# The attention stage of a transformer block: the counted loop over head groups written out as eight bodies in line

## What is computed

```python
mod = jax.nn.silu(condition) @ Wada + bada
sh_a, sc_a, gt_a, sh_m, sc_m, gt_m = jnp.split(mod, 6, axis=1)
xm = layernorm(x, g1, be1) * (1.0 + sc_a[:, None, :]) + sh_a[:, None, :]
x = x + gt_a[:, None, :] * attention(xm, Wqkv, Wproj, bproj)
xm = layernorm(x, g2, be2) * (1.0 + sc_m[:, None, :]) + sh_m[:, None, :]
h = gelu(xm @ W1 + b1)
return x + gt_m[:, None, :] * (h @ W2 + b2)
```

## Time and profile before

| | |
|---|---|
| median of three runs | 2285.84 us (2285.28 to 2287.09) |
| the profiled execution's own time | 2286.51 us |
| its span | 2284.5 us |
| PE busy | 2193.5 us (96% of the span) |
| DVE, ACT, POOL busy | 1293.9, 935.3, 846.0 us |
| mean granted PE clock | 0.978 of full speed |
| attention stage | about 348 to 1451 us of the span |

### The profile page before, as it was taken

The page is one execution under the profiler, slowest core; times in us unless marked ns, Lnnn a source line. Parts: engine busy times, 40 slices in busy tenths (PEclk is TensorE's granted clock), DMA queues, the critical chain, the costliest instruction groups (busy, mean ns, idle before and its releaser), DMA issues. The chain is left out here.

```text
span 2284.5 us, 36721 instructions
## 1 busy us (share of the span) xinstructions
PE 2193.5 (96%) x11550; PEld 1463.3 (64%) x11550; DVE 1293.9 (57%) x2872; ACT 935.3 (41%) x1780; POOL 846.0 (37%) x352
## 2 busy tenths in 40 slices
PE   6999999999999899999999999889999999999998
PEld 5888884444444445444454444577888888888886
DVE  4778876776777667676776765586323133133132
ACT  2111115555556555555555566444422222222221
POOL 2001008667578575785757773581000000000000
PEclk9999999999999999998999999999999999999999
DMA  6547446234261442614326231585211011010010
GB/s 228 208 154 254 145 160 148 48 90 103 53 136 46 92 91 53 149 39 98 79 53 149 50 88 52 181 286 201 92 56 56 0 55 55 0 55 30 25 37 18
DMA packets 129287, 223.46 MB, mean 98 GB/s; under 512 B 8526, under 2 KB 26006, under 8 KB 128920
## 3 DMA queue, kind: packets, MB, share of 16 engines
q1 hardware_dynamic: 107992, 179.38, 28.8%
q10 hardware_dynamic: 21120, 41.95, 5.0%
HBM read 146.31 MB, written 74.98 MB: 97 GB/s over the span
## 5 line engine op out<-in xcount | busy, mean ns | idle before, releaser
L1172 ACT ACTIVATE prob<-st 128x512 f32<-128x512 f32 (+3 forms) x1280 | 613.1, 544 | 431.1 <-PE st L1346 416.4
L1142 POOL TENSOR_TENSOR psum_k<-psum_k,prob 128x2048 f32<-128x2048 f32 x122 | 550.4, 4512 | 42.1 <-ACT prob L1172 34.7
L1228 DVE TENSOR_REDUCE part<-mx 128x1 f32<-128x512 f32 x708 | 435.8, 683 | 132.9 <-PE mx L1326 132.8
L1346 PE MATMUL st<-q_st,k_st 98*128 98x512 f32 (+3 forms) x1280 | 489.2, 397 | 16.5 <-issue 9.0
L1326 PE MATMUL mx<-k_st,qx_st 96*128 96x512 f32 (+3 forms) x1188 | 470.2, 415 | 18.6 <-DVE part L1224 13.3
L1346 PEld LDWEIGHTS st<-q_st,k_st 98*128 98x128 f32 x1280 | 245.7, 193 | 203.8 <-issue 115.5
L1740 DVE TENSOR_TENSOR m_g_lo<-m_g,m_g_hi 128x512 fp32r<-128x512 f32 x128 | 88.7, 693 | 495.3 <-ACT m_g_hi L1654 495.2
L1326 PEld LDWEIGHTS mx<-k_st,qx_st 96*128 96x128 f32 x1188 | 227.1, 192 | 169.2 <-DVE part L1228 96.9
L1224 DVE CUSTOM_DVE_ANT_0 unused<-mx,mask_row 128x128 bf16<-128x128 f32 x480 | 214.0, 488 | 148.7 <-PE mx L1326 131.5
L1363 PE MATMUL o_ps<-prob,v_sb 128*32 128x512 f32 (+3 forms) x2560 | 292.9, 564 | 0.0
L1650 ACT ACTIVATE m_g<-m_hid,vcol 128x512 f32<-128x512 f32 x128 | 88.3, 690 | 480.6 <-PE m_hid L1837 480.6
(11 more groups left out here) (168 smaller groups left out, 2608.1 us busy)
## 6 DMA issues: line engine op xcount, KB each, us to landing
k_st<-qk_scratch SPq DMA_DIRECT2D x96, 256.0 KB, 8.1
qx_st<-qk_scratch SPq DMA_DIRECT2D x96, 256.0 KB, 4.7
q_st<-qk_scratch SPq DMA_DIRECT2D x96, 256.0 KB
qk_scratch<-st_hi ACTq DMA_DIRECT2D x16, 1024.0 KB, 4.2
qk_scratch<-st_lo ACTq DMA_DIRECT2D x16, 1024.0 KB, 6.8
xs<-in_x_dram SPq DMA_DIRECT2D x8, 1024.0 KB, 8.4
v_sb<-v_scratch SPq DMA_DIRECT2D x8, 1024.0 KB, 15.8
o_scratch<-o_sb SPq DMA_DIRECT2D x32, 256.0 KB, 2.3
```

Of the source, the lines that this page charges most:

```text
L1142: nc.gpsimd.tensor_tensor(dst, src, prob[:, s % BUF, :, m:], ALU.add).then_inc(pool_added, 1)
L1172: nc.scalar.activation(prob[:, s % BUF, h, m:], st[n % RING][:, m:], ACT.Exp, scale=SCALE).then_inc(exp_done, 1)
L1228: nc.vector.tensor_reduce(most, bank[:, 0:w], AX.X, ALU.max).then_inc(mx_free, 1)
L1346: nc.tensor.matmul(st[n % RING][:, m:], k_st[u][0:MROWS, h, kt * P:(kt + 1) * P], q_st[0:MROWS, pos % 2, h, m:], start=True, stop=True).th ...
```

## The change

`per_group` no longer builds a loop. All eight bodies are written out one behind the other in every engine's stream, with `g` a constant, and the same `u`, `after` and `more` for each group as before. Nothing else is edited; lines below it are three lower in the changed file.

```diff
         def per_group(eng, body):
 
 
-            body(0, 0, False, True)
-            with eng.Fori(0, NG // 2 - 1) as i:
-                body(2 * i + 1, 1, True, True)
-                body(2 * i + 2, 0, True, True)
-            body(NG - 1, 1, True, False)
+            for g in range(NG):
+                body(g, g % 2, g > 0, g < NG - 1)
```

## The result

| | before | changed |
|---|---|---|
| median | 2285.56 us (2284.68 to 2287.09) | 2265.45 us (2264.21 to 2268.24) |
| ratio, 95% interval | | 0.9912 (0.9898 to 0.9925) |
| profiled execution, own time | 2286.51 us | 2268.24 us |
| its span | 2284.5 us | 2266.5 us |

The change takes 20.1 us off, where 12.0 were forecast. The profiled execution of the changed kernel is the slowest of its four runs, 2.8 us above their median, so the two traces show 18.0 us of the 20.1.

A forecast was written before the change was run, and what follows sets the result against it. PE was taken to bound the kernel, stalling for code at two back edges. Back edges -11.2, loop entry and exit -0.3, registers -0.5 sum to -12.0 us: median 2273.8 us, range 2270.0 to 2279.0.

The forecast's parts named there:

- What bounds the kernel, and where.: Attention: PE sets the pace; groups 3 and 5 stall 4.76 and 4.27 us at back edges, waiting for code.
- the rival that the stall belongs to the place: Start of groups 3 and 5: branch is cheap, the stall stays; 2284.7 us, no change; chance 0.06.
- The two back edges go: -11.2 us.: Groups 3 and 5 each lose 5.6 us, stall and lost clock, against a mean of 138.0; bounds -8.0 to -14.2.
- Nothing in the edit decides which [clock] a group gets.: Attention groups: whether one runs at mean clock 0.98 or 0.96 is untouched by the edit, so the mean was taken.
- The register instructions go: -0.5 us, bounds +0.4 and -1.3.: Groups 1 to 6: register instructions are hidden behind matmuls, at most 0.1 us per group in the mean.
- the sign that I had named: Last three chunks of a group clearly below 78 us at clock 0.98 would show the register instructions had an unseen price.
- The rival that "registers matter more": For example at ends of chunks: registers cost 1 us per group instead of 0.1, another 5.4 us, 2268.4 us; chance 0.02.
- The loop's entry and exit: -0.3 us.: Starts of groups 1 and 7: PE's step falls from 0.45 to 0.31 us, twice; between 0 and that.
- Code in line costs nothing.: Eight bodies instead of four, loaded in the background by the same two queues: no cost; a miss would cost 5.6 us.
- The slower rival: Each of six groups: in-line code arrives late on PE or SP, 5.6 us per group, +22.4 net, 2308.2 us; chance 0.04.

The follow-up runs named there:

- its repeat: The changed kernel, all eight bodies in line with constants, measured once more in a later series: 2265.74 us, ratio 0.9914 to the kernel before.
- the mirror kernel: Against the change: still in line without branches, but ACT, DVE, POOL and SP take groups 1 to 6 from registers, PE has constants; 2265.98 us, ratio 0.9915.

## Why the prediction was wrong

*What bounds the kernel, and where.* Right. PE sets the pace, groups 3 and 5 carry the stall, and it is a wait for code. One argument for it was misread: group 6 is followed by the code of group 7, not by "the same code" as group 0, so only group 0 spoke against the rival that the stall belongs to the place. The kernel with registers and no branch settles it, since its groups 3 and 5 start after 0.43 and 0.42 us.

*"The two back edges go: -11.2 us."* Right in mechanism, somewhat small: 13.6 us by the medians, 13.1 in the profiles. Groups 3 and 5 with registers and without a branch take 137.08 and 137.64 us, not the mean of 138.0 that I set against them. That is 12.5 us, and the other four groups together give the remainder of 0.7. It lies within the bounds I gave (-8.0 to -14.2).

*"Nothing in the edit decides which [clock] a group gets."* Wrong. Over all traces, and leaving out groups 3 and 5 where there is a back edge, 12 of 28 groups are at 0.96 with registers on PE (six kernels) and 5 of 44 with constants (eight kernels). In the change, its repeat and the mirror kernel it is one of 18. How the registers bring the clock down is not shown.

*"The register instructions go: -0.5 us, bounds +0.4 and -1.3."* **This is the step that failed.** They are worth 6.1 us. It failed in two ways, of about the same size. First, I stretched a price from three chunks over the fourth, which no in-line group of the old trace could show, since group 0's first chunk holds the start of the stage; the first chunks hold 3.2 us of the price. Second, I compared only groups of the same clock (0.98), and so left out groups 1 and 4, whose last three chunks take 79.7 and 79.8 us. These lose 1.4 and 1.5 us with the change, and with the registers kept they stay where they were; 2.9 us of the price lie in the last three chunks. So the earlier trace rows were read rightly, and the sign that I had named, a fall clearly below 78 us, did not show, because it looked at the one place and the one clock where the price is not. The term should have been left open over the first chunk, and its bound taken from what a group has there beyond matmuls, 58.71 us of time on 56.22 of PE work, 2.5 us per group. The rival that "registers matter more" had the size nearly right (1 us per group, 5.4 us), though not the place, and only 0.02 of the chance. With it my sum would have been about 2268. Why PE's registers cost at the group's start and at the diagonal tiles, and nowhere else at an equal clock, stays open.

*"The loop's entry and exit: -0.3 us."* Taken from 0.45 against 0.31, as if 0.31 were the floor. The floor is 0.18, since the 0.31 were registers too. Over the six steps that have registers that is about 1.2 us (0.13 to 0.27 each), part of the 6.1.

*"Code in line costs nothing."* Right. No engine has a new wait on "issue" of more than 0.3 us, and fewer packets of code are loaded. The slower rival did not occur, nor the one in which the branch is cheap. The case for PE as the only engine that matters was luckier than it was sound: I had only its wait in view, and ACT's 2.2 and DVE's 3.6 us stood hidden behind it.

The two pages of the Trainium skill divide as the rows had it. The wait for a target outside the loaded code, in the Trainium skill's page "Runtime: NRT & Kernel Launch", "Instruction fetch mechanics", is what the long loop shows, 4.3 to 4.8 us. The 108 ns of the Trainium skill's page "Advanced Engine Details and Errata", "Control Flow Timing", would have given no change; nearest to them comes the short MLP loop, at 0.56 us per pass over code in line, five times as much. That loop does stay loaded: neither code queue of the kernel before has a packet from 1800 to 2100 us, more than three of its passes.

## What to carry to other kernels

A loop whose body is too long to stay loaded pays at each branch back on every engine that runs it, side by side: take one engine's stall away and the next engine's shows, so change all the critical ones together before judging. A loop's price has a second part, the register instructions that its semaphore targets need; here they cost on the engine that sets the pace and on no other, half of it at few places and half through a lower clock. When the trace of before can't show a stretch without the suspected cost, that stretch belongs in the range with an open bound, not under the price of its neighbours. And where the suspected cause may move the clock, a comparison at equal clock leaves out a part of its price.

## What the runs showed of the hardware that was not expected

- At the same back edges PE waited 4.0 to 4.8 us for its code, DVE 3.5 to 3.6 and ACT 2.2 us (each seen where the longer waits had been taken away). POOL's and SP's never reached PE.
- A prefetch hint on the branch cut PE's wait from 4.0 to 4.8 down to 2.4 to 2.8 us, but with hints on all engines ACT then waited 7.59 us on "issue" once the loop had been left, and the sum was no gain.
- A PE register instruction is not free: 689 of them in two bodies, run three times, cost 6 to 7 us in all, some 3 ns each on average with what the clock loses, while those of ACT, DVE, POOL and SP together cost nothing that can be measured.
- One group of the attention took 134.12 us with a mean granted clock of 1.00 (and 134.13 in a second kernel), 2.4 us less than the usual 136.5 with 0.98. No run here tried to bring that about for every group.
- From the end of the attention to the MLP loop the same program text took 210.0 to 211.3 us in eleven kernels and 212.8 to 214.0 in three, with a clock of 0.97 or 0.98 in the first and 0.95 or 0.96 in the second.
